# Deferring twenty quarters of an expert's second products into the next attention, and a symmetric length matrix read once

## The reference, cut to what matters

```python
# attention block (per sequence)
scores = einsum('bhqd,bhkd->bhqk', qt, kt) / sqrt(HD)
attn   = softmax(scores, axis=-1)
out_h  = expmap0(einsum('bhqk,bhkd->bhqd', attn, vt))
attn_out = plin(_from_heads(out_h), w_o, b_o)
...
ff = plin(plin(xm, w_f1, b_f1), w_f2, b_f2)     # plin(x, w, b) = expmap0(logmap0(x) @ w + b)
# mixture of experts (per sequence)
gate_scores = softmax(gate_logits);  topk_w, topk_i = top_k(gate_scores, 2)
for e in the two chosen experts:
    y = gelu(x @ ew1[e] + eb1[e]) @ ew2[e] + eb2[e]
    out += weight(e, token) * y
out += gelu(x @ sw1 + sb1) @ sw2 + sb2           # the shared expert
```

## Time and profile before

| | us |
|---|---|
| median of 3 runs (lowest, highest) | 2297.66 (2296.4, 2298.99) |
| the profiled execution's own time | 2296.17 |
| its span, first to last instruction | 2294.3 |
| busy in the span: PE, DVE, ACT, POOL | 2179.1, 1543.3, 1235.2, 558.5 |

### The profile page before, as it was taken

How to read it: one execution, slowest core, us unless ns; L and a number is a source line. 1 busy time by engine, 2 the same in 40 slices (tenths; PEclk the granted TensorE clock), 3 DMA queues, 4 the chain that set the end, 5 groups by cost and what they waited for, 6 DMA issues and landing times. The chain is left out here.

```text
span 2294.3 us, 93931 instructions
## 1 busy us (share of the span) xinstructions
PE 2179.1 (95%) x38552; PEld 1426.4 (62%) x38552; DVE 1543.3 (67%) x7281; ACT 1235.2 (54%) x4358; POOL 558.5 (24%) x1178
## 2 busy tenths in 40 slices
PE   8899999999999999999989699999999999999999
PEld 6677777777777777777763246464646556464666
DVE  5777777778777787777874776674848475674520
ACT  4555555555555555555556564756565564656422
POOL 0222122242222422223223132222213032222100
PEclk9999999999999999999999799999999999999999
DMA  4111111101000000000001322313230222313020
GB/s 121 33 39 36 39 32 39 48 27 32 23 27 29 27 30 25 27 30 27 13 28 54 83 79 37 134 38 134 37 111 23 58 113 37 134 37 106 1 88 10
DMA packets 111007, 117.28 MB, mean 51 GB/s; under 512 B 69604, under 2 KB 92516, under 8 KB 106484
## 3 DMA queue, kind: packets, MB, share of 16 engines
q1 hardware_dynamic: 107172, 108.75, 15.6%
q10 hardware_dynamic: 3408, 2.52, 0.4%
HBM read 75.53 MB, written 21.04 MB: 42 GB/s over the span
## 5 line engine op out<-in xcount | busy, mean ns | idle before, releaser
L135 PE MATMUL psFI<-wh,Hs 128*8 128x128 f32 (+3 forms) x8192 | 324.6, 276 | 59.9 <-DVE Hs L250 46.8
L135 PE MATMUL psOR<-wh,RH 128*16 128x128 f32 (+3 forms) x8320 | 321.1, 272 | 2.8 <-ACT RH L338 2.2
L135 PEld LDWEIGHTS psFI<-wh,Hs 128*8 128x8 f32 (+3 forms) x8192 | 182.2, 99 | 177.5 <-DVE Hs L250 177.5
L2023 ACT ACTIVATE pexp<-bank 128x1024 f32<-128x1024 f32 x256 | 244.2, 1022 | 47.6 <-PE bank L1369 47.4
L338 ACT ACTIVATE RH<-RT 128x16 f32<-128x16 f32 x512 | 110.8, 216 | 260.9 <-DVE RT L254 260.9
L1263 PE MATMUL bank<-x3T,ew 128*128 128x512 f32 x512 | 238.0, 592 | 0.0
L234 DVE STREAM_TRANSPOSE FIT<-psFI 128x128 f32<-128x128 f32 x512 | 162.1, 317 | 101.0 <-PE psFI L135 98.3
L329 ACT ACTIVATE sFI<-FIT 128x32 f32<-128x32 f32 x512 | 118.6, 232 | 200.1 <-DVE FIT L234 195.2
L135 PEld LDWEIGHTS psOR<-wh,RH 128*16 128x16 f32 (+1 forms) x8320 | 205.5, 104 | 5.3 <-ACT RH L338 3.8
L135 PE MATMUL psG<-wh,Hs 128*8 128x64 f32 (+3 forms) x8192 | 208.3, 219 | 0.0
L1277 PE MATMUL bank<-ew,hidden 128*128 128x256 f32 x864 | 201.0, 379 | 0.0
(11 more groups left out here) (366 smaller groups left out, 4064.3 us busy)
## 6 DMA issues: line engine op xcount, KB each, us to landing
ew<-in_ew SPq DMA_DIRECT2D x32, 1024.0 KB, 9.5
qkv_scratch<-qkvr SPq DMA_DIRECT2D x31, 384.0 KB, 2.9
big<-qkv_scratch SPq DMA_DIRECT2D x7, 1536.0 KB, 7.8
XX<-in_xT SPq DMA_DIRECT2D x31, 256.0 KB, 2.6
x_scratch<-xr SPq DMA_DIRECT2D x32, 128.5 KB, 2.4
x<-x_scratch SPq DMA_DIRECT2D x8, 514.0 KB, 9.1
ada<-ada_scratch SPq DMA_DIRECT2D x8, 512.0 KB, 8.6
out_x<-x SPq DMA_DIRECT2D x7, 512.0 KB, 3.4
```

What stands on the lines that cost most here:

```text
L135: last = pe.matmul(bank[32 * j:32 * j + width, :], state(k), weights[:, k, j, cols], start=False, stop=k == KC - 1, tile_position=(0, 32 * ...
L2023: up(act.activation(M.pexp[:, n % 2, 2 * pr:2 * pr + 2, :], M.PS[pr][:, :, :], ACT.Exp, scale=1.0 / math.sqrt(HD)), "exps")
```

## The change

Six steps (18 to 23) of sequence e-1 no longer finish where they were. Steps 18 and 19 do the quarters of tokens 0 to 255 in the expert phase, as before three steps behind; all else, 4 x 2 + 6 x 2 = 20 quarters, goes to the next attention. In iterations n = 0 to 3 one quarter stands ahead of `scores(n+1)` and one between its two pairs; in n = 4 to 14 one stands between the two pairs, and in n = 15 one ahead of `values(15)`. The last sequence (round 8 has no attention) has the 20 quarters in a row at its start.

What follows from it: `hidden` has 8 slots instead of 5 and takes the memory of the feed-forward weights (used in round 0 only); bank 7 is occupied during the attention, so all `back` and the gate use bank 6, and `back(g)` waits for the copy of group g-1; `last_outputs` is in two halves, the second after `oT_moved(3)`; x3 and the token weights are double; SP stores x3 between the loads of the two chosen experts in the next round. `up(0)` moves behind `output_transposes(0)`, one of its two matmuls ahead of `back(3)` and one behind it.

Apart from that: G is symmetric, so the matrix is laid out as [G's first 128 columns, w_f1·w_f2, G's last 128], the second accumulating matmul of L1478 starts at column 128 (384 columns instead of 512), and the block of G left out is doubled in the other one.

```diff
-LEAD, HIDDEN, IN_NEXT = 3, 5, STEPS - 3
+LEAD, HIDDEN = 3, FC
+WHOLE, HALVES = STEPS - 6, STEPS - 4
+FIRST_HALF, SECOND_HALF = (0, 1), (2, 3)
...
-        self.hidden = sb("hidden", [P, HIDDEN, T])
+        self.hidden = self.W["wf"]
...
+    def down_in_half(i, tiles, e=e):
+        n, m = divmod(i, FC)
+        pe.wait_ge(*at("hidden", e, i + 1))
+        for q in tiles:
             last = pe.matmul(M.y_bank(q), M.hidden[:, i % HIDDEN, q * P:(q + 1) * P], M.expert(n)[1][:, m, :], start=False, ...)
+        if i == STEPS - 1 and q == tiles[-1] and q in (FIRST_HALF[-1], SECOND_HALF[-1]):
+            last.then_inc(M.sem("y_last"), 1)
+    second_halves = [(i, q) for i in range(WHOLE, STEPS) for q in SECOND_HALF]
...
     def steps(lo, hi):
-            if i >= LEAD and i % FC != LEAD:
+            if i >= LEAD and i % FC != LEAD and (i - LEAD < WHOLE or e == NB - 1):
                 down(i - LEAD)
+            elif WHOLE <= i - LEAD < HALVES:
+                down_in_half(i - LEAD, FIRST_HALF)
...
     def scores(n, batch=b, between=()):
         for pr in range(2):
+            if pr:
+                for i, q in between:
+                    down_in_half(i, (q,), e - 1)
...
     def back(g, tiles=range(NQ)):
+        if g == 0 and e >= 1:
+            pe.wait_ge(*at("l_max", e))
-        if g >= 2:
-            pe.wait_ge(*at("O", b, g - 1))
+        if g >= 1:
+            pe.wait_ge(*at("O", b, g))
-            last = pe.transpose(bank(6 + g % 2)[...], M.oT[...], I[:, :])
+            last = pe.transpose(bank(6)[...], M.oT[...], I[:, :])
...
-            if e >= 1:
-                down_of_last(last_three[3 * n:3 * n + 3])
+            between = []
+            if e >= 1 and n < STEPS - HALVES:
+                down_in_half(HALVES + n, FIRST_HALF[:1], e - 1)
+                between = [(HALVES + n, FIRST_HALF[1])]
+            elif e >= 1:
+                between = [second_halves[n - (STEPS - HALVES)]]
             if n + 1 < len(units):
-                scores(n + 1)
-            elif experts:
-                up(0)
+                scores(n + 1, between=between)
+            else:
+                for i, q in between:
+                    down_in_half(i, (q,), e - 1)
...
         output_transposes(0)
+        if experts:
+            up(0, (0,))
         back(H // 4 - 1)
+        if experts:
+            up(0, (1,))
...
-                last = pe.matmul(bank(q), M.zT[...], M.gram[:, k, :], ...)
+                last = pe.matmul(bank(q)[:, k * P:], M.zT[...], M.gram[:, k, k * P:], ...)
...
         for s, ei in enumerate(index):
+            if s and e:
+                sp.wait_ge(*at("x3_out", e - 1))
+                sp.dma_start(out[e - 1]..., M.x3s[(e - 1) % 2][:, :, :]).then_inc(M.sem("out"), 16)
             sp.dma_start(M.ew1[s][:, :, :], ...)
...
-    elif experts:
-        sp.wait_ge(*at("x3_out", e))
-        sp.dma_start(out[e]..., M.x3[:, :, :]).then_inc(M.sem("out"), 16)
```

More of the change, by code:

```diff
@@ L1217, in place @@
         self.gidx, self.g6, self.b6 = sb("gidx", [1, 8], u32), sb("g6", [1, 3 * TOPK]), sb("b6", [P, 3 * TOPK])
-        self.wm = sb("wm", [P, TOPK, NQ])
+        self.wms = [sb(f"wm_{par}", [P, TOPK, NQ]) for par in range(2)]
     def of_heads(self, name, batch, n=None):
@@ L1249, in tensor_round, with up @@
     at = lambda name, round_, n=None: M.sig[name].at(round_, n)
-    def up(i):
+    def up(i, halves=range(KC)):
         n, m = divmod(i, FC)
@@ L1261, in up @@
             pe.wait_ge(*at(f"ew_in_{n - 1}", e))
-        for k in range(KC):
-            last = pe.matmul(bank(4 + i % 2), M.expert(n)[0][:, k, m * P:(m + 1) * P], M.x3T[:, k, :], start=k == 0, stop=k == KC - 1)
-        last.then_inc(M.sem("eup"), 1)
+        for k in halves:
+            last = pe.matmul(bank(4 + i % 2), M.expert(n)[0][:, k, m * P:(m + 1) * P], M.x3T[:, k, :], start=k == 0, stop=k == KC - 1, skip_group_check=True)
+        if k == KC - 1:
+            last.then_inc(M.sem("eup"), 1)
     def down(i, e=e):
@@ L1268, in down @@
         pe.wait_ge(*at("hidden", e, i + 1))
[L1269 to L1272, removed]
+        if i == 0:
+            if front:
+                pe.wait_ge(*at("O", b))
+            if e:
+                pe.wait_ge(*at("x3_out", e - 1))
         elif m == 0:
@@ L1326, in gram @@
         for m in range(FC):
-            last = pe.matmul(bank(4 + k), W["wf"][:, m, D + k * P:D + (k + 1) * P], W["wf"][:, m, :], start=m == 0, stop=m == FC - 1)
+            last = pe.matmul(bank(4 + k), W["wf"][:, m, 3 * P * k:3 * P * k + P], W["wf"][:, m, :], start=m == 0, stop=m == FC - 1)
         last.then_inc(M.sem("gram_ps"), 1)
@@ L1357, in tensor_round, with scores @@
     units = [(g, kc) for g in range(H // 4) for kc in range(NQ)]
-    def scores(n, batch=b):
+    def scores(n, batch=b, between=()):
         g, kc = units[n]
         for pr in range(2):
+            if pr:
+                for i, q in between:
+                    down_in_half(i, (q,), e - 1)
             if n:
@@ L1460, in tensor_round @@
     else:
-        for i in range(IN_NEXT, STEPS):
-            down(i, e - 1)
+        for i in range(HALVES, STEPS):
+            down_in_half(i, FIRST_HALF, e - 1)
+        for i in range(WHOLE, STEPS):
+            down_in_half(i, SECOND_HALF, e - 1)
         steps(0, 2)
@@ L1467, in tensor_round @@
         steps(5, STEPS)
-        for i in range(IN_NEXT, STEPS - 2):
+        for i in range(STEPS - LEAD, STEPS - 2):
             down(i)
@@ L1477, in tensor_round @@
             for k in range(KC):
-                last = pe.matmul(bank(q), M.zT[:, k, q * P:(q + 1) * P], M.gram[:, k, :], start=k == 0, stop=k == KC - 1)
+                last = pe.matmul(bank(q)[:, k * P:], M.zT[:, k, q * P:(q + 1) * P], M.gram[:, k, k * P:], start=k == 0, stop=k == KC - 1, skip_group_check=True)
             last.then_inc(M.sem("ff_ps"), 1)
@@ L1580, in expert_biases, with last_outputs @@
         for q in range(NQ):
-            Gc.link(dve.scalar_tensor_tensor(M.x3[:, q, :], M.eb2[0][:, :], M.wm[:, 0, q:q + 1], M.x3[:, q, :], ALU.mult, ALU.add))
+            Gc.link(dve.scalar_tensor_tensor(x3[:, q, :], M.eb2[0][:, :], wm[:, 0, q:q + 1], x3[:, q, :], ALU.mult, ALU.add))
         dve.wait_ge(Gc.sem, Gc.n)
         for q in range(NQ):
-            up(dve.scalar_tensor_tensor(M.x3[:, q, :], M.eb2[1][:, :], M.wm[:, 1, q:q + 1], M.x3[:, q, :], ALU.mult, ALU.add), "x3_bias")
-    def last_outputs(e):
+            up(dve.scalar_tensor_tensor(x3[:, q, :], M.eb2[1][:, :], wm[:, 1, q:q + 1], x3[:, q, :], ALU.mult, ALU.add), "x3_bias")
+    def last_outputs(e, tiles=range(NQ)):
         dve.wait_ge(*at("y", e))
[L1589 to L1593, removed]
+        last, x3, wm = e == NB - 1, M.x3s[e % 2], M.wms[e % 2]
+        for q in tiles:
+            if last:
+                dve.wait_ge(*at("edown", e, STEPS - 1 + q))
+            elif q % 2 == 0:
+                dve.wait_ge(*at("y_last", e, q // 2 + 1))
+            up(dve.scalar_tensor_tensor(x3[:, q, :], (M.last_bank if last else M.y_bank)(q), wm[:, 1, q:q + 1], x3[:, q, :], ALU.mult, ALU.add), "x3_out")
     def statistics(N, xa, qs):
@@ L1814, in vector_round @@
         if e:
-            last_outputs(e - 1)
+            last_outputs(e - 1, FIRST_HALF if front else range(NQ))
     if experts and front:
@@ L1818, in vector_round @@
             oT_moved(0)
-        gate_logits(7)
+        gate_logits(6 if e else 7)
     elif experts:
@@ L1835, in vector_round @@
         if experts:
-            token_weights(7)
+            token_weights(6 if e else 7)
             move_x3()
@@ L1846, in vector_round @@
         oT_moved(3)
+        if e >= 1:
+            last_outputs(e - 1, SECOND_HALF)
         o_moved(3)
@@ L1900, in linear_outputs @@
             dve.wait_ge(C.sem, C.n)
[L1901 removed]
+            halves = lambda t: t.rearrange("p (a c) -> p a c", c=P)
+            C.link(dve.tensor_tensor_reduce(out=halves(M.dump_dve[:, :]), in0=halves(z[:, q, :]), in1=halves(bank(q))[:, 0::3, :], scale=1.0, scalar=S[:, 9, q:q + 1],
                                             op0=ALU.mult, op1=ALU.add, accum_out=acc[:, 7, q:q + 1]))
[L1903 removed]
+            up(dve.tensor_tensor(M.w[:, q, :], bank(q)[:, P:P + D], M.ff_rows[:, 0:D], ALU.add), "ff_bias")
         for q in range(NQ):
@@ L1951, in outputs @@
         for q in range(NQ):
-            up(act.activation(M.weighted[:, q, :], M.y_bank(q), ACT.Identity, scale=M.wm[:, 0, q:q + 1] if n else 1.0), "y_act")
+            up(act.activation(M.weighted[:, q, :], M.y_bank(q), ACT.Identity, scale=M.wms[e % 2][:, 0, q:q + 1] if n else 1.0), "y_act")
     def squares(src, sums, where, q, raises=None):
@@ L2004, in gram_moved @@
         act.wait_ge(*at("gram_ps", b, k + 1))
-        up(act.copy(M.gram[:, k, :], bank(4 + k)), "gram")
+        if k:
+            up(act.copy(M.gram[:, k, P:], bank(4 + k)[:, P:]), "gram")
+            return
+        up(act.copy(M.gram[:, k, 0:3 * P], bank(4 + k)[:, 0:3 * P]), "gram")
```

(6 more changed lines are left out.)

50 lines of the change are left out of this document (23 added, 27 removed).

## The result

The changed kernel takes 2306.2 us (median of 6 runs, 2305.28 to 2308.04), against 2298.44 for the kernel before in the same job: so 7.8 us slower by the medians. The recorded ratio is 1.0039, 95% interval 1.0028 to 1.0050, which is 9.0 us (6.4 to 11.5). The profiled execution spans 2304.4 us, 10.1 more than the one before.

What follows compares the result with a forecast made beforehand. PE was taken as the bound. Rounds 2 to 7 add 6 x 1.33 = +8.0 us, round 1 -1.7, round 8 +2.65, round 0 nothing: +8.9, taken as +8.5, giving 2306 us; range 2299 to 2312.

Steps and rivals of the forecast that it cites:

- A visit costs 0.20, and 0.29 between the pairs: PE, attention: full-array fp32 matmuls among strips cost 0.20 us extra per visit, plus 0.09 for breaking a pair of scores.
- The wait for the last gelu: PE, round start: with the whole down gone, 0.93 of its 1.73 us becomes a wait ahead of the transposes.
- The sum told otherwise: Second tally of a round: surcharge 5.35 us instead of 0.80, against some 3.5 idleness and 0.86 matrix, 0.3 net new wait.
- Start: Step from the last up to the end of attention unit 0, including waits for gelu and first exponential: -0.3 us.
- DVE's slack behind the attention: The copy on DVE's chain from the gate's second visit would hold 1.3 us of slack before back(3).
- Last outputs at no cost: DVE behind the attention: the second half, two operations of 0.42 us, fits in the slack; without it up to 0.85.
- SP: Store and second expert's load move to about 1604, needed 55 us behind 1600.39 and landing in some 10: no cost.
- Rounds 0, 1 and 8: Separately priced rounds: round 0 at 0 (-0.9 to +0.5), round 1 at -1.7, round 8 at +2.65 us.
- the covered quarter: Attention rival: weights load while scores stream, so a quarter costs only its bare 0.43 us; near 2282, chance 0.11.
- The free break of the pairs: Attention rival: splitting a pair of scores costs nothing, 8.1 us less; 2298, no change; chance 0.10.
- DVE taking over behind the attention: Rival: last_outputs delays o_moved(3) and following transposes, up to 6 us, 2312; beyond 2312 shares 0.05 with the surcharge-only rival.
- deferral alone would cost 2325: Rival: deferral just moves work without idleness to fill, surcharge alone +4.5 us a round; shares 0.05 with DVE beyond 2312.

Runs made afterwards that it cites:

- e1: The kernel before with only the shorter, symmetric length matrix product and its layout, no quarter deferred: 2290.13 us against 2296.49, ratio 0.9973.
- e3: The changed kernel with each unit's quarter ahead of the next unit's scores instead of between its two pairs: 2288.3 us, ratio 0.9967 to the kernel before.
- d1: The changed kernel with 56 added full-array fp32 matmuls of 128 columns, one ahead of each up(5) to up(12), rounds 1 to 7: spans 13.0 us more.
- d3: As d1, but each added fp32 matmul stands on one strip of 32 columns of the array: spans 30.3 us more than the changed kernel.
- e4: The changed kernel with the first half of step 20 left in the expert phase, 18 quarters deferred instead of 20: 2300.11 us, ratio 1.0015.
- e5: The kernel of e3 with each half down of steps 18 and 19 one step later: 2282.5 us against 2296.83 for the kernel before, ratio 0.9937.
- e2: The changed kernel with the product 512 columns wide again, so the deferral stands alone: 2312.19 us, ratio 1.0069 to the kernel before.
- e6: The kernel of e5 with the twelve second-half quarters in six visits of two, directly following a back: 2290.73 us, ratio 0.9973 to the kernel before.
- d2: As d1, but each added matmul is one fp16 instruction on the full array: spans 7.0 us more than the changed kernel.

## Why the prediction was right

The sign, the size and the mechanism came out: 2306.2 was predicted and measured. The agreement to a tenth of a us is luck. The kernel before had 2297.66 when the prediction was made and 2298.44 in the job of the result; the difference there is 7.8 us by medians, where 8.5 was predicted, and the two profiled spans differ by 10.1.

Step by step, in round 3 (predicted, then measured as differences of starts, from the end of the last up in each trace, before 1557.71, after 1556.38 + 1.72 = 1558.10):

| step | predicted | measured |
|---|---|---|
| to the end of unit 0, with the wait for the gelu | -0.3 | -0.37 (6.12 instead of 6.49) |
| units 1 to 3 | -0.45 | -0.38 (1564.22 to 1572.92, 8.70 for 9.08) |
| units 4 to 14 | +5.0 | +5.15 (1572.92 to 1600.57, 27.65 for 22.50) |
| unit 15 | -1.2 | -1.29 (1.52 for 2.81) |
| to the next up | +0.9 | +0.85 (2.65 for 1.80) |
| half downs of steps 18, 19 | -1.73 | -1.73 (each 0.86, as 1555.52 to 1556.38, for 1.73) |
| the product | -0.86 | -0.85 (e1) |
| a round | +1.3 to +1.4 | +1.39 |

- *A visit costs 0.20, and 0.29 between the pairs.* Right. The rows of the changed kernel and e3 show the size, and d1 to d3 that it comes with the tiling. The prediction's sentence that each inserted quarter adds two changes of tiling holds only between the pairs. Ahead of the scores the tiling changes anyway, from strips of 32 columns to halves of the rows, so that a quarter there adds one; the price it was given, 0.20, was read from the rows and is right. What I hadn't used is that a quarter next to a `back` shares its visit; the rows for that stood in the trace of before (the `back` has a surcharge of its own). The prediction was hardly hurt, as only unit 15's quarter touches a `back` in the changed kernel (its visit took 0.53 and not 0.63); the expectation of e3 was.
- *The wait for the last gelu.* Predicted 0.93, measured 0.94 (1558.10 to 1559.04), of which the profile calls 0.78 idle; e4 and e5 show that work of 0.86 fits into it.
- *The sum told otherwise.* The second way in which the prediction adds up a round doesn't come out: its terms give 4.55 - 3.5 - 0.86 + 0.3 = +0.5, not +1.3. The term that is too small is the last one. The idleness that the change brings is the wait of 0.94 ahead of the transposes, and in unit 0 a wait for the first exponential of 0.72 instead of 0.24: 1.4 in all, not 0.3. The first sum, step by step, has these inside its *Start* and is right. The forecast was taken from it.
- *DVE's slack behind the attention.* I gave `back(3)` 1.3 us. The copy it needs ended at 1603.08 (start 1602.45), 0.36 ahead of it. The chain on DVE is itself paced by PE now: `o_moved(2)` at 1600.77 waited 0.75 for `back(2)`, whose second part starts at 1600.30, 13.76 behind the gate's second visit, where it was 11.07 in the kernel before. My slack counted from the gate's visit and left that wait out. It held, but barely; by the times of e4 it no longer did there.

```profile
1600.77 0.69 DVE L1794 COPY spl<-bank 128x512 f32<-128x512 f32 x1 [0.75 <-PE bank L1407]
...
1602.45 0.63 DVE L1790 COPY spl<-bank 128x512 f32<-128x512 f32 x1
1603.00 0.86 DVE L1619 SCALAR_TENSOR_TENSOR x<-bank,wm,x 128x256 f32<-128x256 f32 x2
1604.08 0.69 DVE L1794 COPY spl<-bank 128x512 f32<-128x512 f32 x1 [0.23 <-PE bank L1407]
```

- *Last outputs at no cost.* Right: the two operations at 1603.00 (L1619) end before `o_moved(3)` at 1604.08, which waits for PE.
- *SP.* Right: the store and the second expert's load go out at 1603.88 and 1604.49 (1604 predicted), and no expert matmul waits for them.

```profile
1603.88 0.40 SPq L2227 DMA_DIRECT2D out_x<-x  x1
1604.49 0.35 SPq L2228 DMA_DIRECT2D ew<-in_ew  x1
```

- *Rounds 0, 1 and 8.* Round 8 from its first transposes to the end takes 3.6 more (8 quarters, 3.45). Round 1, from its transposes to those of round 2, takes 2.4 less (0.96 more in its first part, 3.36 less in its second); the prediction's -1.7 counts only to the last up, ahead of the 0.8 that the next start saves, so it agrees. Without round 0 this comes to -2.4 + 6 x 1.39 + 3.6 = +9.5 where the prediction's pieces give +8.9. The 0.4 that it took off for longer waits on DVE has nothing behind it: rounds 2 to 7 of the kernel before are alike to 0.02 us. The transposes of round 1 come 0.6 later, which I can't assign: the kernels of this study that have the same round 0 as the changed one stand between -0.1 and +2.3 there.

The rivals: the covered quarter (2282) is out, no visit of a lone quarter among strips cost under 0.63. Nor were weights loaded ahead there: those of the quarter at 1565.18 started at 1565.17, while those of d1's added matmul at 1623.05, among full-array work, started at 1622.83. The free break of the pairs (2298) is out by e3, where 0.09 a unit came back. DVE taking over behind the attention (over 2312) is out, as `o_moved(3)` waited 0.23 for PE. That deferral alone would cost 2325 is out by e2: 2312 with the wide product.

## What to carry to other kernels

Idle time of the bounding engine is not free space: price what fills it at its place, by start-to-start times of such neighbours, borders included. On PE, count visits rather than matmuls when full-array work goes among tiled work; put it next to other full-array work rather than between two matmuls of one tiling (e3), and still spread it so that the engine fed by the tiled part isn't starved (e5 against e6). And when deferred work leaves a gap, look at what had been hiding behind it.

## What the runs showed of the hardware

- A change of TensorE's tiling costs some 0.1 us at each side, for fp32 as for the fp16 scores. Of a lone quarter in the changed kernel the first instruction takes 0.33 (1564.22 to 1564.55) and the second 0.31 (to 1564.86), where each takes 0.22 within full-array work. An fp16 pair ahead of a quarter takes 0.32, ahead of another pair 0.21 (0.53 less 0.32). In d3 the down ahead of the strip lasted 0.09 longer (1.82 for 1.73), the strip's two instructions 0.12 longer (0.34 for 0.22), and the up behind it 0.10 (1.82 for 1.72). The Trainium skill (TensorEngine Tiling (Array Packing), "Tiling Modes") says that such a change drains TensorE. The trace agrees as far as it shows: at these borders the work ahead gets longer and no weights are loaded ahead.

```profile
1564.55 0.38 PE L1299 MATMUL bank<-ew,W_wf 128*128 128x256 f32 x1
```

- Within one tiling, fp32 to fp16 and back cost 0.11 with the matmul itself (d2), about half of that the fp16 instruction's own 0.06.
- The price of a lone quarter hardly varies: of the changed kernel's 114 quarters that have scores behind them, 108 took 0.63 or 0.64 us from their start to the scores'; the other six, one a round in unit 0, waited for an exponential.
